# Three edits to a fused transformer kernel on one core: later transposed tokens in the inner pipeline, another job order in the first attention, a routing product over 128 rows

## The chip, the cores and the metric

The kernel runs on one core of one Trainium2 chip. A core has TensorE (PE, with its weight loads listed as PEld), VectorE (DVE), ScalarE (ACT), GpSimdE (POOL) and a queue for transfers (SP); each runs its own list of instructions in order and they wait for each other through semaphores. The metric is the device time in microseconds (us) of one execution, the median of three runs.

## The reference

Input `x` is 16 batches of 256 tokens by 128 features. All arithmetic is float32. Two outer layers are computed, each as `x = x + s * silu(g)` after a layernorm `xn` of `x`:

```
# layer 0
s = sliding_window_attention(xn)   # 16 heads of 8, window 64, each token sees its block of 64 and the one before, ALiBi-like bias
g = moe(xn)                        # 8 experts of 176, top 2 of a softmax router, plus a shared expert of 352: silu(x wg) * (x wu) @ wd
# layer 1
s = attention(xn)                  # 16 heads of 8, all 256 keys, a relative bias
g = inner(xn)                      # depth 2, each: shift tokens, local attention (8 heads of 64, window 64, rotary, l2-normed q and k),
                                   #   x = x + o @ wo;  h = layernorm(shift(x)) ; x = x + (a * gelu(b)) @ w2 + b2,  a, b = split(h @ w1)
```

## The kernel before

The program is a row of blocks, one after the other, each with an instruction list for every engine: `load_inputs`, `layernorm`, `router`, `head_attention("a0")`, `experts`, `layernorm`, `head_attention("a1")`, `inner_layers`, `finish`. At the end of a block the engines meet. The change touches three of them. In all three the order of every engine's work is written out by hand as a loop over steps, and `k` in "step s handles item s + k" is a lookahead.

**First attention (`a0`, windowed).** A batch of 256 tokens has two tiles of 128 tokens, and a tile has two units of 8 heads, so there are 4 steps a batch and 64 units in all. For each unit PE computes `score`, DVE adds the bias table (line 700) and takes row maxima (706), POOL subtracts them (508), ACT takes the exponent (667), PE transposes the probabilities (576), ACT copies them to SBUF (672), and PE sums values and denominators (602, 609). Scores run 4 units ahead, for two units in every even step. DVE normalises a tile (711, 713) in each odd step. Beside that stream stand small jobs that all go through one PSUM bank, bank 7: `x` (transpose the tokens of a batch, 532), `qk` (project queries and keys, 536), `v` (project values, 542) and one `y` for each tile (output projection, 547). Every job must have been copied out by ACT (643, 648, 649, 658, 662) before PE may begin the next one; this is `after(pe, aux_free, n)`. POOL expands the keys of a batch (`mask_keys`, 501) from ACT's copy before PE scores it. `x` and `qk` of a batch stand two batches ahead of its units. In an even step PE does `qk` or `v` ahead of `score`; `y` stands last in an odd step, so the next job, first in the following even step, comes right behind it.

**Experts.** 8 rounds of 512 tokens. The 1760 features are cut into 14 slices `s` (11 routed, 3 shared). For a slice PE does a gate product and an up product of three matmuls each (817, 818, 819: high and low parts in fp32r), then for the 11 routed slices one matmul (848) that spreads the routing weights `wT` (24 rows by 512 tokens, bf16) over the slice's features with the selection matrix `sel16` (24 rows by 1408). The down product of slice s-2, again three matmuls, follows. DVE multiplies (953, 957), ACT splits off the high part (919), POOL the low part (932) that the down product waits for. In slice 8 PE also transposes the next round's tokens (825), which ACT copies (890) ahead of its next high part; in slice 10 it transposes the next routing weights (831, 128 by 24 each), which ACT copies too (894). ACT makes `sel16` once, at the block's start (886).

**Inner layers.** 64 tile steps (2 layers of 32 tiles). In a step PE does `score` (1249), the query and key projection of the tile 5 ahead (1214 to 1216), `transpose_out` (1283), `transpose_prob` (1258), the value projection (1222 to 1224) after it has waited for DVE's `add_mask` of the same step, `tokens` (1202), `project_out` (1289), sometimes `mlp_out` (1312), `sums` (1273) and `transpose_qk` (1233), and at the end one chunk of the feed-forward's first product (1303). A feed-forward round R covers four tiles and is spread over the steps 4R+6 to 4R+13. In step 4R+7 DVE computes `deviations(R)` (1578 to 1585, the normalised tokens `mn`), PE transposes them at the very end of the same step (`mlp_tokens`, 1295, into bank 0), and DVE scales them into `mT` (`keep_mlp_tokens`, 1593), also in that step. In step 4R+8 the first chunk follows, last on PE. The query and key projection uses banks 0 and 1 too, and so waits for `m_sb`.

```
R, c = round_at(step, 8)          # PE, end of a step
if R is not None and c < NC:
    projections_taken(pe, step)
    if not is_tile(step + LEAD):
        banks_01_free(pe, step)
    mlp_chunk(R, c)
R, c = round_at(step, 7)
if R is not None and c == 0:
    ...
    mlp_tokens(R)
```

## Time and profile before

| | |
|---|---|
| median of 3 runs | 1960.74 us (1957.76 to 1961.09) |
| profiled execution | 1958.84 us, its span 1956.5 us |
| busy in the span | PE 1619.0 (83%), PEld 1187.8 (61%), DVE 1375.9 (70%), ACT 1183.4 (60%), POOL 1087.8 (56%) |
| DMA | 40.16 MB, mean 21 GB/s |

Read it by blocks, since their limits differ. Seen in the timeline, the first attention runs from 96 to 348 us, the experts from 348 to 678 us, the second attention from 701 to 1102 us and the inner layers from there to 1937 us. The span is one execution as the profiler saw it; the profiled execution's own time is some 2 us above it.

### The profile page before, as it was taken

How to read it: one execution, taken by the hardware profiler on the slowest of the kernel's cores; microseconds unless marked ns; L12 is line 12 of the kernel's file. 1: busy time of each engine (PE TensorE's matmuls, PEld its weight loads, DVE VectorE, ACT ScalarE, POOL GpSimd, SP SyncE). 2: the span in 40 equal slices, each digit the busy share in tenths (PEclk: the TensorE clock that was granted, in tenths of full speed). 3: DMA queues.
4: the chain of work that ended last, by engine and by line, in shares of the span. 5: the costliest groups of instructions: out<-in, count | busy, mean ns of one | idle time of the engine just before them, and what ended most of it. 6: DMA issues, size and time to landing. Idle time of an engine off the chain costs nothing. (4 is left out here: it accounts for less than half of the span.)

```text
span 1956.5 us, 47756 instructions
## 1 busy us (share of the span) xinstructions
PE 1619.0 (83%) x18705; PEld 1187.8 (61%) x18705; DVE 1375.9 (70%) x2187; ACT 1183.4 (60%) x1972; POOL 1087.8 (56%) x632
## 2 busy tenths in 40 slices
PE   0479999699999739999999668888888999888863
PEld 0346666466666527677777447666666777666742
DVE  4468887444554569999999588877777777777633
ACT  0147767444444327777777558777777777777742
POOL 0166665244444327777776677666666666666413
PEclk9999999899999959999999879999999998999986
DMA  3010000000000140000000001111111111111101
GB/s 104 2 48 3 3 3 3 14 13 7 6 7 6 29 133 2 2 2 2 3 2 2 10 15 32 23 23 23 23 24 24 23 23 23 23 26 24 23 21 43
DMA packets 52210, 40.16 MB, mean 21 GB/s; under 512 B 24408, under 2 KB 44028, under 8 KB 51876
## 3 DMA queue, kind: packets, MB, share of 16 engines
q1 hardware_dynamic: 52004, 37.28, 7.4%
q8 instruction: 145, 2.38, 0.5%
q14 instruction: 61, 0.50, 0.1%
HBM read 15.68 MB, written 2.13 MB: 9 GB/s over the span
## 5 line engine op out<-in xcount | busy, mean ns | idle before, releaser
L508 POOL TENSOR_TENSOR a_prob<-a_prob,a_top 128x1024 f32<-128x1024 f32 x192 | 359.7, 1894 | 133.1 <-DVE a_top L706 133.1
L700 DVE TENSOR_TENSOR a_prob<-ps,a_table 128x1024 f32<-128x1024 f32 x192 | 226.2, 1220 | 70.6 <-PE ps L562 47.8
L932 POOL TENSOR_TENSOR e_hh<-e_h,e_hh 128x512 fp32r<-128x512 f32 x112 | 144.2, 1290 | 195.4 <-ACT e_hh L919 193.7
L672 ACT ACTIVATE a_probT<-ps 128x1024 f32<-128x1024 f32 x192 | 196.5, 1023 | 90.0 <-PE ps L576 89.9
L706 DVE TENSOR_REDUCE a_top<-a_prob 128x4 f32<-128x1024 f32 (+1 forms) x192 | 225.2, 1215 | 8.7
L576 PEld LDWEIGHTS ps<-ident,a_prob 128*128 128x128 f32 x1536 | 168.0, 141 | 95.5 <-issue 60.1
L667 ACT ACTIVATE a_prob<-a_prob 128x1024 f32<-128x1024 f32 x192 | 202.7, 1056 | 33.0 <-POOL a_prob L508 33.0
L576 PE MATMUL ps<-ident,a_prob 128*128 128x128 f32 x1536 | 208.9, 279 | 7.8 <-ACT a_probT L672 2.9
L1170 POOL TENSOR_TENSOR i_qk<-i_qk,i_rn 128x1024 f32<-128x1024 f32 x64 | 123.3, 1927 | 117.7 <-DVE i_rn L1498 117.7
L1157 POOL TENSOR_TENSOR i_qk<-i_raw,i_rot 128x1024 f32<-128x1024 f32 x64 | 152.0, 2375 | 47.8 <-issue 42.6
L953 DVE TENSOR_TENSOR e_h<-ps,e_sg 128x512 f32<-128x512 f32 x112 | 77.4, 691 | 143.7 <-PE ps L819 118.3
L902 ACT ACTIVATE e_sg<-ps 128x512 f32<-128x512 f32 x112 | 66.9, 597 | 160.0 <-PE ps L819 160.0
L1412 ACT ACTIVATE i_prob<-i_prob,i_top 128x128 f32<-128x128 f32 x512 | 156.3, 394 | 9.8 <-DVE i_top L1507 8.0
L1160 POOL TENSOR_TENSOR i_qk<-i_qk,i_rt 128x1024 f32<-128x1024 f32 x64 | 151.3, 2365 | 19.4 <-DVE i_rt L1515 12.4
L602 PE MATMUL ps<-a_probT,a_V 128*32 128x64 f32 (+1 forms) x4096 | 159.5, 250 | 1.7 <-DVE a_oT L713 1.5
L1377 ACT ACTIVATE i_raw<-ps 128x1024 f32<-128x1024 f32 x64 | 65.6, 1025 | 154.5 <-PE ps L1216 154.4
L609 PE MATMUL ps<-a_probT,a_ones 128*32 128x128 f32 x3072 | 154.3, 273 | 0.0
L602 PEld LDWEIGHTS ps<-a_probT,a_V 128*32 128x32 f32 x4096 | 90.6, 109 | 33.7 <-issue 31.0
L501 POOL TENSOR_TENSOR a_kM<-a_kT,a_own 128x1024 f32<-128x1024 f32 x32 | 60.6, 1894 | 69.9 <-ACT a_kT L651 52.7
L817 PE MATMUL ps<-e_xT,e_wgu_hi 128*128 128x512 f32 x224 | 91.3, 408 | 4.7 <-DVE e_wd_lo L977 4.7
L1515 DVE TENSOR_TENSOR i_rt<-ps,i_rot 128x512 f32<-128x512 f32 x128 | 82.1, 683 | 15.1 <-ACT i_raw L1377 14.9
L1303 PE MATMUL ps<-i_mT,i_w 128*128 128x512 f32 (+1 forms) x192 | 90.6, 594 | 2.2 <-DVE i_A L1600 2.2
(213 smaller groups left out, 3830.9 us busy)
## 6 DMA issues: line engine op xcount, KB each, us to landing
i_V<-i_V SPq DMA_DIRECT2D x96, 130.0 KB, 2.3
a_table<-skew_scratch SPq DMA_DIRECT2D x2, 2048.0 KB, 12.9
X<-in_L_attn_x SPq DMA_DIRECT2D x4, 512.0 KB, 6.3
a_table<-in_c_l_table SPq DMA_DIRECT2D x1, 2048.0 KB, 8.1
e_xs<-Y SPq DMA_DIRECT2D x8, 256.0 KB, 2.3
i_ms<-Y SPq DMA_DIRECT2D x16, 128.0 KB
out_dram<-X SPq DMA_DIRECT2D x4, 512.0 KB, 3.3
i_ms<-Y SPq DMA_DIRECT2D x16, 127.0 KB
```

What stands on the lines that cost most here:

```text
L508: nc.gpsimd.tensor_tensor(s, s, top[:, slot].unsqueeze(2).broadcast_to([P, HG, KW]), ALU.subtract).then_inc(shifted, 1)
L576: last = nc.tensor.transpose(ps[:, 4 + b // 4, (b % 4) * P:(b % 4 + 1) * P], flat[:, b * P:(b + 1) * P], ident[:, :])
L602: nc.tensor.matmul(ps[32 * g:32 * g + 32, 6, cols], vals[:, 32 * x:32 * x + 32], src[:, at + cols.start:at + cols.stop], start=(first and ...
L609: last = nc.tensor.matmul(ps[32 * g:32 * g + 32, 6, P:2 * P], ones[:].rearrange("p x d -> p (x d)")[:, 32 * x:32 * x + 32], src[:, at:at + ...
L667: nc.scalar.activation(s, s, ACT.Exp).then_inc(exped, 1)
L672: nc.scalar.activation(probT[:, n % 4].rearrange("p (b n) -> p b n", b=2), ps[:, 4:6, :], ACT.Copy).then_inc(pT_sb, 1)
L700: nc.vector.tensor_tensor(prob[:, slot].rearrange("p (b x) k -> p b x k", b=2), ps[:, 2 * (n % 2):2 * (n % 2) + 2, :].rearrange("p b (x k) ...
L706: nc.vector.tensor_reduce(top[:, slot], prob[:, slot], AX.X, ALU.max).then_inc(max_done, 1)
L932: nc.gpsimd.tensor_tensor(hh[0:n, b % HBUF, 1, :], h[0:n, b % HBUF, :], hh[0:n, b % HBUF, 0, :].bitcast(F32), ALU.subtract).then_inc(h_lo, 1)
L1157: nc.gpsimd.tensor_tensor(s, raw[:, T % 2], cosines, ALU.mult).then_inc(cos_done, 1)
L1160: nc.gpsimd.tensor_tensor(s, s, rt[:], ALU.add).then_inc(rotated, 1)
L1412: last = nc.scalar.activation(s, s, ACT.Exp, bias=top[:, T % 2, h:h + 1])
```

## The change

**First attention.** The shared function is split in two, `window_attention` for `a0` and `bias_attention` for `a1`; the latter issues what it did. In `window_attention` the jobs `x` and `y` become one job `xy` in each batch's slot for `x`: it transposes the tokens of batch i and does the output projection of both tiles of batch i-4, in different halves of bank 7. ACT copies both, the second as one piece of 256 columns. `oT` has four buffers in place of two. In a step, PE now does `score` ahead of the job, and ACT the exponent ahead of the job's copies.

**Experts.** `ws`, `wT` and `sel16` are 128 rows (or columns) wide in place of 24, the rest of them zero; POOL clears `ws` and `sel16` at the block's start, and the first transfers and ACT's copy wait for that. The routing product is over 128 rows, of which 104 are zero. `ws` is filled by the same transfers, now into strided rows.

**Inner layers.** `mlp_tokens` moves from the end of step 4R+7 to step 4R+8, between `mlp_out` and `sums`; `keep_mlp_tokens` moves on DVE to step 4R+8, between `add_mlp` and `quotient`. The wait of the next projection for `m_sb` goes.

```diff
+def window_attention(nc, name, t, ps, ident, Y, S):
...
-        oT = sb("oT", [P, 2, P])
+        oT = sb('oT', [P, 4, P])
...
-        AT = {"x": -7, "qk": -6, "v": 0} if windowed else {"x": -7, "qk": -6, "v": -3}
-        JOBS = sorted([(i * U + AT[kind], 0, kind, i, 0) for i in range(NBATCH) for kind in AT]
-                      + [((T + 1) * NU + 3, 1, "y", T // TPB, T % TPB) for T in range(TILES)])
+        AT = {'xy': -7, 'qk': -6, 'v': 0}
+        DELAY = 4
+        LAST = (NBATCH + DELAY - 1) * U + AT['xy'] + 1
+        JOBS = sorted([(i * U + AT[kind], kind, i) for i in range(NBATCH) for kind in AT] + [(i * U + AT['xy'], 'xy', i) for i in range(NBATCH, NBATCH + DELAY)])
...
+                if kind == 'xy':
+                    if i < NBATCH:
+                        for k in range(TPB):
+                            last = nc.tensor.transpose(ps[:, 7, k * P:(k + 1) * P], Y[:, i * TPB + k, :], ident[:, :])
+                    if i >= DELAY:
+                        for k in range(TPB):
+                            T = (i - DELAY) * TPB + k
+                            pe.wait_ge(o_sb, T + 1)
+                            last = nc.tensor.matmul(ps[:, 7, (2 + k) * P:(3 + k) * P], oT[:, T % 4, :], wT[:, 3, :], start=True, stop=True)
...
+            for step in range(FIRST, LAST):
+                if step % 2 == 0 and 0 <= step + AHEAD < UNITS:
+                    score(step + AHEAD)
+                for n, kind, i in jobs_at(step):
+                    job(n, kind, i)
+                if 0 <= step < UNITS:
+                    transposes(step)
+                if 0 <= step - 2 < UNITS:
+                    sums((step - 2) // 2, step % 2)
...
-        sel16 = sb("sel16", [3 * NE, ROUTED], BF16)
+        sel16 = sb("sel16", [P, ROUTED], BF16)
-        ws = sb("ws", [P, 4, 3 * NE])
+        ws = sb("ws", [P, 4, P])
-        wT = sb("wT", [3 * NE, 2, N], BF16)
+        wT = sb("wT", [P, 2, N], BF16)
...
-                sp.dma_start(ws[:], wparts[:, bass.ds(i * 4, 4), :]).then_inc(staged, 16)
-
+                sp.dma_start(ws[:, :, 0:3 * NE], wparts[:, bass.ds(i * 4, 4), :]).then_inc(staged, 16)
+
+            sp.wait_ge(cleared, 2)
...
+            nc.gpsimd.memset(ws[:], 0.0).then_inc(cleared, 1)
+            nc.gpsimd.memset(sel16[:], 0.0).then_inc(cleared, 1)
...
-            R, c = round_at(step - 1, 7)
-            if R is not None and c == 0:
-                eng.wait_ge(m_sb, R + 1)
...
+                R, c = round_at(step, 8)
+                if R is not None and c == 0:
+                    projections_taken(pe, step)
+                    if not is_tile(step + LEAD):
+                        banks_01_free(pe, step)
+                    mlp_tokens(R)
                 if is_tile(step - 1):
                     sums(step - 1)
...
-                R, c = round_at(step, 7)
-                if R is not None and c == 0:
-                    projections_taken(pe, step)
-                    if not is_tile(step + LEAD):
-                        banks_01_free(pe, step)
-                    mlp_tokens(R)
...
+                R, c = round_at(step, 8)
+                if R is not None and c == 0:
+                    keep_mlp_tokens(R)
                 if is_tile(step - 1):
                     quotient(step - 1)
```

PE in the first attention before, at the middle of the batches: `a_wT,a_oT` is a `y`, `a_xT,a_wT` a `qk`, `a_kM,a_qT` a score, `ident,a_prob` the transposed probabilities, the last two names the sums.

```order
L609 MATMUL ps<-a_probT,a_ones 32x128 x4
L547 MATMUL ps<-a_wT,a_oT 128x128
L536 MATMUL ps<-a_xT,a_wT 128x256 x2
L562 MATMUL ps<-a_kM,a_qT 64x512 x8
L576 MATMUL ps<-ident,a_prob 128x128 x8
L602 MATMUL ps<-a_probT,a_V 32x64 x8
```

The `xy` job on PE in the changed kernel (`ident,Y` and `a_wT,a_oT` with two products), with the step's transposes and the first of its sums behind it.

```order
L505 MATMUL ps<-ident,Y 128x128 x2
L510 MATMUL ps<-a_wT,a_oT 128x128 x2
L539 MATMUL ps<-ident,a_prob 128x128 x8
L559 MATMUL ps<-a_probT,a_V 32x64 x8
L563 MATMUL ps<-a_probT,a_ones 32x128 x4
```

The `qk` job in the next step of the changed kernel, between the last sum of the step ahead and the first of its own.

```order
L563 MATMUL ps<-a_probT,a_ones 32x128 x4
L531 MATMUL ps<-a_kM,a_qT 64x512 x8
L513 MATMUL ps<-a_xT,a_wT 128x256 x2
L539 MATMUL ps<-ident,a_prob 128x128 x8
L559 MATMUL ps<-a_probT,a_V 32x64 x8
```

The output projection no longer stands right before another job: transposes, sums and a score lie between `xy` and `qk`.

PE in the inner layers before, from the end of step 4R+7 (`ident,i_G` is `mlp_tokens`) into step 4R+8; `i_qkT` is the score, `i_mT,i_w` the feed-forward's chunk.

```order
L1289 MATMUL ps<-i_wo,i_oT 128x128 x4
L1273 MATMUL ps<-i_V,i_probT 64x65 x16
L1233 MATMUL ps<-ident,i_qk 128x128 x8
L1295 MATMUL ps<-ident,i_G 128x128 x4
L1249 MATMUL ps<-i_qkT 64x128 x16
L1214 MATMUL ps<-i_w_hi,i_h_hi 128x512
```

The end of step 4R+8 on PE in the changed kernel.

```order
L1494 MATMUL ps<-i_wo,i_oT 128x128 x4
L1517 MATMUL ps<-i_w,i_A 128x128 x6
L1500 MATMUL ps<-ident,i_G 128x128 x4
L1478 MATMUL ps<-i_V,i_probT 64x65 x16
L1438 MATMUL ps<-ident,i_qk 128x128 x8
L1508 MATMUL ps<-i_mT,i_w 128x512 x2
```

`mlp_tokens` has moved past the score, both projections, `transpose_out`, `transpose_prob`, `project_out` and `mlp_out` of the next step, and stands two groups ahead of the chunk that needs it.

DVE in the same steps, in the changed kernel, from the last of `deviations` (`i_G`) over `add_mask` (`i_prob`) to the scaled tokens (`i_mT`), which stood right behind `i_G` before.

```order
L1790 TENSOR_SCALAR i_G<-i_ms,i_mv,i_rstd 128x128 x4
L1699 SCALAR_TENSOR_TENSOR i_rtmp<-i_ss,i_rn 128x32
L1701 TENSOR_TENSOR i_rtmp<-i_rtmp,i_rn 128x32
L1703 SCALAR_TENSOR_TENSOR i_rn<-i_rtmp,i_rn 128x32
L1728 TENSOR_REDUCE i_ss<-i_sq 128x16
L1709 TENSOR_TENSOR i_prob<-ps,i_mask 128x1024
L1712 TENSOR_REDUCE i_top<-i_prob 128x8
L1720 TENSOR_TENSOR i_rt<-ps,i_rot 128x512 x2
L1749 CAST i_h_hi<-ps 64x128
```

Behind these stand three more writes of the token parts, the two additions to `Y`, and then `i_mT`, ahead of the reciprocal of `quotient`.

## Rows read from the trace of the kernel before

**Rows 1.** Busy time by stretch: start:end, length, then busy us (instructions) of each engine, PEclk, DMA share, GB/s.

```profile
96.00:348.00 252.00, 225.53 (x4388) 157.14 (x4388) 187.76 (x192) 164.17 (x274) 155.55 (x88) 0.99 0.04 12
...
363.00:676.00 313.00, 296.91 (x1181) 196.08 (x1181) 151.77 (x221) 138.11 (x246) 144.22 (x112) 0.99 0.02 6
...
1140.00:1900.00 760.00, 659.95 (x7067) 523.15 (x7067) 572.35 (x1163) 560.76 (x1082) 464.59 (x244) 0.95 0.11 24
```

**Rows 2.** Timeline of PE and ACT, first attention: start, us, engine, line [idle before].

```profile
202.46 1.16 PE L542 MATMUL ps<-a_wT,a_xT 128*128 128x128 f32 x8 [0.37 <-ACT S L662]
...
216.12 0.49 PE L547 MATMUL ps<-a_wT,a_oT 128*128 128x128 f32 x2
216.64 0.28 ACT L662 ACTIVATE S<-ps 128x128 f32<-128x128 f32 x1 [0.41 <-PE ps L547]
...
216.97 1.16 PE L542 MATMUL ps<-a_wT,a_xT 128*128 128x128 f32 x8 [0.37 <-ACT S L662]
...
218.06 1.11 PE L562 MATMUL ps<-a_kM,a_qT 32*64 32x512 f32 x16
```

**Rows 3.** Timeline of DVE in the same two steps.

```profile
214.49 2.35 DVE L706 TENSOR_REDUCE a_top<-a_prob 128x8 f32<-128x1024 f32 x2
...
216.75 0.95 DVE L711 RECIPROCAL a_rden<-ps 128x128 f32<-128x128 f32 x1
...
217.77 0.29 DVE L713 TENSOR_TENSOR a_oT<-ps,a_rden 128x128 f32<-128x128 f32 x1
...
219.28 2.36 DVE L700 TENSOR_TENSOR a_prob<-ps,a_table 128x1024 f32<-128x1024 f32 x2 [1.22 <-PE ps L562]
```

**Rows 4.** Timeline of PE around a routing product of the experts.

```profile
382.66 0.39 PE L819 MATMUL ps<-e_xT,e_wgu_lo 128*128 128x512 f32 x1
...
382.98 0.39 PE L848 MATMUL ps<-e_wT,e_sel 24*128 24x512 bf16 x1
...
383.29 0.50 PE L817 MATMUL ps<-e_hh,e_wd_hi 128*128 128x512 f32 x1
...
383.63 0.39 PE L818 MATMUL ps<-e_hh,e_wd_hi 128*128 128x512 f32 x1
```

**Rows 5.** Timeline of PE and PEld, inner layers, fp32r to float32 of equal shape.

```profile
1428.39 0.39 PE L1224 MATMUL ps<-i_w_hi,i_h_lo 128*128 128x512 f32 x1
1428.39 0.14 PEld L1202 LDWEIGHTS ps<-ident,Y 128*128 128x128 f32 x1
...
1428.62 0.27 PE L1202 MATMUL ps<-ident,Y 128*128 128x128 f32 x1
```

**Rows 6.** Timeline of PE, experts: the down product of slice 9.

```profile
389.11 0.50 PE L817 MATMUL ps<-e_hh,e_wd_hi 128*128 128x512 f32 x1 [0.16 <-POOL e_hh L932]
```

**Rows 7.** Groups by line, 1140 to 1900 us: count, busy, mean ns, idle before.

```profile
L1295 PE MATMUL ps<-ident,i_G 128*128 128x128 f32 x60 | 13.1, 357 | 53.4 <-DVE i_G L1585 53.4
```

**Rows 8.** Timeline of PE and DVE, inner layers, into and through step 4R+8.

```profile
1411.13 0.68 PE L1295 MATMUL ps<-ident,i_G 128*128 128x128 f32 x4 [4.21 <-DVE i_G L1585]
1411.74 1.99 PE L1249 MATMUL ps<-i_qkT 64*64 64x128 f32 x32
1411.85 0.81 DVE L1593 TENSOR_SCALAR i_mT<-ps,i_vecs 128x512 f32<-128x512 f32 x1 [0.86 <-PE ps L1295]
...
1414.52 1.21 DVE L1504 TENSOR_TENSOR i_prob<-ps,i_mask 128x1024 f32<-128x1024 f32 x1
...
1416.98 0.48 PE L1222 MATMUL ps<-i_w_hi,i_h_hi 128*128 128x512 f32 x1
...
1420.46 0.28 DVE L1544 CAST i_h_hi<-ps 64x128 fp32r<-64x128 f32 x1 [2.17 <-PE ps L1312]
...
1421.96 0.41 DVE L1606 TENSOR_TENSOR Y<-ps,Y 128x256 f32<-128x256 f32 x1
...
1422.21 1.88 PE L1303 MATMUL ps<-i_mT,i_w 128*128 128x512 f32 x4
```

**Rows 9.** Timeline of PE after a shorter wait, inner layers.

```profile
1153.12 0.50 PE L1222 MATMUL ps<-i_w_hi,i_h_hi 128*128 128x512 f32 x1 [2.53 <-DVE i_prob L1504]
```

More of the change, by code:

```diff
@@ L380, in _ @@
                     dve.drain()
[L383 to L385 removed]
+def window_attention(nc, name, t, ps, ident, Y, S):
+    KW = 2 * WIN
     HG = 1024 // KW
@@ L439, in jobs_at @@
-        def jobs_at(step, place):
-            return [(n, kind, i, tile) for n, (s, p, kind, i, tile) in enumerate(JOBS) if (s, p) == (step, place)]
-        def job_of(kind, i, tile=0):
-            return [j[2:] for j in JOBS].index((kind, i, tile)) + 1
+        sb = lambda n, s: c.enter_context(nc.sbuf_tensor(name + '_' + n, s, F32))
+        sem = lambda n: c.enter_context(nc.semaphore(name + '_' + n))
+        wnat = sb('wnat', [P, 4, P])
+        wT = sb('wT', [P, 4, P])
+        own = sb('own', [P, QG])
@@ new lines, in _, with add_bias, row_max, normalise @@
+        @block.vector
+        def _(dve):
+            dve.wait_ge(b_loaded, NBL)
+            dve.wait_ge(zeroed, NZERO)
+            def add_bias(n, slot):
+                i, tile, pair, half = unit(n)
+                dve.wait_ge(scores, n // 2 + 1)
+                after(dve, p_T, n - NBUF + 1)
+                heads = table[:, tile].rearrange('p (g x) k -> p g x k', x=QG)
+                nc.vector.tensor_tensor(prob[:, slot].rearrange('p (b x) k -> p b x k', b=2), ps[:, 2 * (n % 2):2 * (n % 2) + 2, :].rearrange('p b (x k) -> p b x k', k=KW), heads[:, 2 * half:2 * half + 2, XX * pair:XX * (pair + 1), :], ALU.add).then_inc(biased, 1)
+            def row_max(n, slot):
+                nc.vector.tensor_reduce(top[:, slot], prob[:, slot], AX.X, ALU.max).then_inc(max_done, 1)
+            def normalise(T):
+                dve.wait_ge(pv, (T + 1) * NU)
+                after(dve, aux_ps, job_of('xy', T // TPB - 2 + DELAY) if T >= 4 else 0)
+                nc.vector.reciprocal(rden[:, :], ps[:, 6, P:2 * P])
+                dve.drain()
+                nc.vector.tensor_tensor(oT[:, T % 4, :], ps[:, 6, 0:P], rden[:, :], ALU.mult).then_inc(o_sb, 1)
+                dve.drain()
+            def job(n, kind, i):
+                dve.wait_ge(aux_ps, n + 1)
+                split = lambda a: a.rearrange('p (g x d) -> p g x d', g=4, x=QG)
+                for k in range(TPB):
+                    last = nc.vector.tensor_tensor(V[:, i % 2, 0, k, :, :, 0:D], split(ps[:, 7, k * P:(k + 1) * P]), split(bvo[:, 0, :]), ALU.add)
+                last.then_inc(aux_free, 1)
+            for step in range(FIRST, LAST):
+                T, r = divmod(step - 1, NU)
+                n = step + AHEAD
+                if r == 0 and 1 <= T <= TILES:
+                    normalise(T - 1)
+                if step % 2 == 0 and 0 <= n < UNITS:
+                    add_bias(n, n % NBUF)
+                    add_bias(n + 1, (n + 1) % NBUF)
+                dve.drain()
+                if step % 2 == 0 and 0 <= n < UNITS:
+                    row_max(n, n % NBUF)
+                    row_max(n + 1, (n + 1) % NBUF)
@@ L540, in job @@
                             at = PAD + P * k - WIN * v
[L541 to L543 removed]
+                            rows = xR[:, par, at:at + P]
+                            last = nc.tensor.matmul(ps[:, 7, (v * TPB + k) * P:(v * TPB + k + 1) * P], rows, wT[:, 2, :], start=True, stop=True)
                 else:
@@ L682, in _ @@
                     keep_probT(step)
-                if windowed:
-                    for n, kind, i, tile in jobs_at(step, 1):
-                        job(n, kind, i, tile)
         @block.vector
@@ L730, in _ @@
                     normalise(T - 1)
-                if not windowed:
-                    for a, kind, i, tile in jobs_at(step, 1):
-                        job(a, kind, i, tile)
+                for a, kind, i, tile in jobs_at(step, 1):
+                    job(a, kind, i, tile)
                 n = step + AHEAD
@@ L737, in _ @@
                     add_bias(n + 1, (n + 1) % NBUF)
-                if not windowed:
-                    for a, kind, i, tile in jobs_at(step, 0):
-                        if kind == "v":
-                            job(a, kind, i, tile)
+                for a, kind, i, tile in jobs_at(step, 0):
+                    if kind == 'v':
+                        job(a, kind, i, tile)
                 dve.drain()
```

442 lines of the change are left out of this document (289 added, 153 removed).

## The prediction

> **What bounds the kernel now.** I began with the page: PE is busy 83% of the span, no other engine above 70%. The chain that ended last says little here, since its rows cover 1% of the span. So I asked for busy time by stretch [rows 1] and then read the timeline inside each block that the change touches. In the first attention PE is busy 225.53 of 252.00 us and in the experts 296.91 of 313.00, both at a granted clock of 0.99. DVE, the next one, has 187.76 and 151.77. These blocks go at PE's pace, and what is to be looked for is time that PE loses between its instructions. In the inner layers PE has 659.95 of 760.00 us at a clock of 0.95; there it waits for others at certain places, and one has to find who sets the end of a round of four steps.
>
> **First attention: the end of a wait.** `y` starts at 216.12, ACT copies it at 216.64 for 0.28 us, and PE's next job `v` starts at 216.97 [rows 2]. From start to start that is 0.85 us. The four products of `v` take 216.97 to 218.06, 0.27 us each, and `y` is one product of that kind. So 0.58 us are a wait for one copy, in every odd step, ahead of `v` or `qk`. In the changed order a whole step's transposes and sums lie behind `xy`, and a score too, so the copy is hidden. `y`'s two products stay. Of the 32 `y` jobs 27 have a job right behind them (tiles 0 to 25 and 27); the batch period, 202.46 to 216.97, is 14.51 us and should become 14.51 - 2 x 0.58 = 13.35.
>
> Does another engine stop that? DVE needs for two steps 2.36 + 2.35 + 0.95 + 0.29 us and about 0.1 of gaps, 6.05 us in all, and now waits 1.22 us for scores [rows 3]. The batch of 13.35 us holds two such pairs, 12.1, so DVE fits with 1.2 us left. The pair with `qk` is the shorter one on PE (it has no `xy`), about 6.4 us: still over 6.05. POOL has 155.55 us of 252 [rows 1] and fits. What gets later is the key expansion: `qk` now stands behind a score (some 1.1 us, [rows 2]), and the scores that need the keys stand first in their step and no longer behind the 1.09 us of `v`. That eats about 2.2 us of a lead of a whole pair of steps less POOL's expansion, so I cost it at nothing in the steady part, but at the start, where PE has no lead, at 1.4 us. The last `xy` adds a product and a longer copy, 0.4 us. Sum: 27 x 0.58 - 1.8 = 13.9; **-14 us**. Bounds: the waits come back in part as waits of DVE's kind, -6; nothing is lost at the start and the gaps between array shapes shrink as well, -18.
>
> **Experts: the routing product.** A stream of 512-column matmuls runs at 0.23 us from start to start, as 1428.39 to 1428.62 shows [rows 5]. Around the routing product it is 382.66, 382.98, 383.29, 383.63 [rows 4]: 0.97 us for three, where 0.69 would do. 0.28 us are lost each time. Nothing is waited for; the load for the routing product starts only when the stream ahead is through, and so does the next one's. Which property of it does that, the 24 rows or bf16? Rows 5 show a change of type at equal shape, fp32r to float32: the load of 1202 starts at 1428.39, together with the matmul ahead of it, and costs nothing. Rows 4 differ from that in shape and in bf16. I take the shape, with bf16 as the open part: no row has a bf16 product over 128 rows. There are 8 x 11 = 88 such products: 88 x 0.28 = 24.6 us.
>
> The Trainium skill has a rule on each side. TensorEngine Tiling (Array Packing), Tiling Modes, says that a change of tiling mode, not just of tile, drains the engine, and 24 rows fall in a mode of 32; by it the whole 24.6 us go, and rows 4 agree. TensorE: Matmul & The Clock Gate, section LDWEIGHTS, says that a load with 32 rows takes as long as one with 128 and that only columns count; read alone, it makes the edit worth 0. That is a rival below.
>
> Some of it is given back where PE then meets POOL's low part. The down product of slice 9 waits 0.16 us already [rows 6]: ACT copies the next tokens ahead of its high part, and this copy depends on PE's transposes in slice 8. They stand right behind a routing product, so they come only 0.32 + 0.31 - 2 x 0.23 = 0.17 us earlier, while the down product would come 2 x 0.28 = 0.56 earlier. I take 0.4 us a round there, 0.2 for the like of it with the routing weights in slice 10 and 11 (the transposes of 128 columns in place of 24 included), over 7 rounds 4 us. The two clears at the start, the strided transfer and ACT's wait for the clears cost nothing: from the block's start at 348 to the first product at 363 [rows 1] the engines split the expert weights, and the tokens are wanted only behind that. Should that cover be gone, they cost some 2 us, once. Sum: **-21 us**, bounds 0 and -25.
>
> **Inner layers: the moved transposes.** PE stood 53.4 us before line 1295 in 15 rounds, waiting for DVE [rows 7]. It is tempting to book them all. Rows 8 show one round. `mlp_tokens` starts at 1411.13 after a wait of 4.21. DVE then scales at 1411.85 for 0.81, and only at 1412.66 goes on with the norms and square sums of the next step; `add_mask` is over at 1415.73, and the value projection, which needs it, starts at 1416.98. With the edit DVE goes on at 1411.1, so `add_mask` is over at 1415.73 - 1.55 = 1414.2. PE has the score, the projection and both transposes behind it long before (they were free from 1407 on; 4 us of work at full clock) and waits for `add_mask` in place of the tokens. So the value projection starts at 1414.3 in place of 1416.98, 2.65 us earlier. DVE's part of it (1544 at 1420.46, 1606 at 1421.96 to 1422.37) follows at the same distance: over at 1419.7. Now comes what was put off: the scaled tokens take 0.81 us more here, to 1420.6, and the chunk at 1422.21 needs them. PE itself is ready at 1422.21 - 2.65 + 0.5 (the transposes put in) = 1420.1. The chunk starts at 1420.7: 1.5 us gained a round, and DVE's `quotient` behind it gains as much. 15 rounds: **-22 us**. Bounds: -40 if the scaled tokens are no limit (2.65 x 15); 0 if the chunk's wait and the later `quotient` eat it.
>
> **The sum** is -14 - 21 - 22 = -57 us against the profiled execution's 1958.84, that is 1901.8. The median of the runs shown, 1960.74, lies 1.9 above it: 1903.7, say **1904 us**.
>
> **Rivals.**
> 1. *The routing product gains nothing*, because bf16 or the length of a load is what costs, not the rows. For it: no row shows bf16 at 128 rows. Against it: rows 5. 1904 + 21 = 1925 us.
> 2. *The inner wait only moves.* PE's 4.21 us turn into the wait for `add_mask` plus the one for the scaled tokens, and the round keeps its length. For it: the chunk is within 0.6 us of a DVE-set time in my own account. 1904 + 22 = 1926 us.
> 3. *Slower, through the clock.* The wait of 4.21 us is followed by a score of 1.99 us [rows 8], at the lower level, 1.2 GHz; a wait of 2.53 us is followed by a matmul of 0.50 us, still at 2.4 GHz [rows 9]. In the changed step PE waits some 2.6 us for `add_mask`, right ahead of the longest stretch of products on the path. If that wait drops the clock, value projection to chunk, 1422.21 - 1416.98 + 0.5 = 5.7 us at full clock, doubles: 5.7 - 1.5 = 4.2 us lost a round, +63. With the other blocks' -35 that is 1961 + 28 = 1989 us. It turns the kernel slower from a loss of 35 / 15 = 2.3 us a round on.
> 4. *The inner round gains the full 2.65*, or more as the clock stays up: 1904 - 18 = 1886 us.
>
> **How the numbers follow.** The forecast, all three parts within a few us (1890 to 1915), 0.55; rival 1 0.14; rival 2 0.14; rivals 1 and 2 together (1947) 0.02; rival 3 0.05; rival 4 0.10. About 0.2% (4 us) is what a measurement of this kernel can tell from no change. The range goes from 1885 to 1927 and leaves out the double failure, rival 3 and some of the ends: below 0.2. Faster by over 0.2%: all but rival 3 and a bit of the double failure, 0.94; same 0.01; slower 0.05. The forecast's own range is 1890 to 1915.
>
> **What the changed profile would show.** First attention: `v` and `qk` without an idle ahead of them, and a batch of 13.3 to 13.5 us; if 14 or more, look at DVE ahead of its bias addition and at PE ahead of the score, for the keys. Experts: 0.23 us on both sides of the routing product, and a wait of about 0.5 us for POOL in slice 9; if 0.32 stays, rival 1 holds. Inner layers: no wait before the token transposes, one of 2 to 3 us before the value projection of step 4R+8, and about 0.5 before the chunk; a round of 46.5 us. If the value projection there has matmuls well above the 0.48 us of rows 8, the clock has dropped, and rival 3 is at work. The prediction is wrong if a block's gain is missing, which each of these rows tells by itself.

## The result, and the profile after

The changed kernel takes 1907.31 us (median of 4 runs, 1906.76 to 1909.29), the one before 1960.91 (4 runs beside it): ratio 0.9732, 95% interval 0.9715 to 0.9748. The profiled execution took 1909.29 us with a span of 1907.2.

The blocks follow from where each one's first instruction stands in the two traces: the first attention is 17.7 us shorter, the experts 19.8, the layer norm and second attention 0.5 longer, the inner layers 12.1 shorter. Sum 49.1 of the spans' 49.3. The forecast had 14, 21 and 22.

Busy time by stretch of the kernel after, the answer to [rows 1] (start:end, length, busy us and instructions of PE, PEld, DVE, ACT, POOL, clock, DMA share, GB/s):

```profile
96.00:330.00 234.00, 215.68 (x4388) 156.78 (x4388) 189.11 (x192) 161.97 (x258) 155.02 (x88) 1.00 0.04 13
345.00:639.00 294.00, 276.87 (x1168) 198.37 (x1183) 151.73 (x222) 140.04 (x246) 144.03 (x112) 0.99 0.02 7
1103.00:1863.00 760.00, 659.29 (x7084) 521.72 (x7085) 576.55 (x1179) 567.02 (x1087) 467.56 (x246) 0.96 0.11 24
```

In the inner layers PE is as busy in 760 us as before. A shorter round should have put more work into them.

**First attention**, timeline of PE in the kernel after, against [rows 2]:

```profile
203.69 0.40 PE L563 MATMUL ps<-a_probT,a_ones 128*32 128x128 f32 x8
204.02 1.11 PE L531 MATMUL ps<-a_kM,a_qT 32*64 32x512 f32 x16
205.07 1.13 PE L513 MATMUL ps<-a_xT,a_wT 128*128 128x256 f32 x4
206.03 1.04 PE L539 MATMUL ps<-ident,a_prob 128*128 128x128 f32 x8
...
211.28 1.16 PE L518 MATMUL ps<-a_wT,a_xT 128*128 128x128 f32 x8
...
214.26 0.44 PE L505 MATMUL ps<-ident,Y 128*128 128x128 f32 x2
214.53 0.61 PE L510 MATMUL ps<-a_wT,a_oT 128*128 128x128 f32 x4
```

No wait stands ahead of `qk` (L513), `v` (L518) or the joint job (L505 and L510). The score stands right behind the sums, and the job right ahead of the transposes. From score to score a batch takes 6.21 + 6.74 = 12.95 us. It was 14.51, and the forecast said 13.35.

**Experts**, timeline of PE around a routing product (L1052) in the kernel after, with that product's load (PEld), against [rows 4]:

```profile
351.70 0.40 PE L1023 MATMUL ps<-e_xT,e_wgu_lo 128*128 128x512 f32 x1
351.93 0.10 PEld L1052 LDWEIGHTS ps<-e_wT,e_sel 128*128 128x128 bf16 x1 [0.28 <-issue]
351.94 0.39 PE L1052 MATMUL ps<-e_wT,e_sel 128*128 128x512 bf16 x1
351.98 0.58 PE L1021 MATMUL ps<-e_hh,e_wd_hi 128*128 128x512 f32 x1
352.39 0.40 PE L1022 MATMUL ps<-e_hh,e_wd_hi 128*128 128x512 f32 x1
```

From L1023 to L1022 it is 0.69 us, where the same three gaps took 0.97 before. How they split (0.24, 0.04, 0.41) is odd, but the sum is that of an unbroken stream, as forecast. The load of the routing product still starts only with its own product (351.93 beside 351.94) and not with the one ahead of it, so a load that is not issued ahead is not enough to cost time. The wait for POOL in slice 9, forecast at about 0.5 us, is 0.25 (0.16 before). The give-back that it was to explain came all the same: an undisturbed round of 14 slices went from 38.84 to 36.40 us, 2.44 where eleven routing products save 11 x 0.27 = 3.0. Where the difference goes was not traced.

**Inner layers**, timeline of PE through a step 4R+8 of the kernel after, against [rows 8]; the first two lines are from the same place one round earlier:

```profile
1232.54 1.06 PE L1494 MATMUL ps<-i_wo,i_oT 128*128 128x128 f32 x8
1233.43 1.50 PE L1517 MATMUL ps<-i_w,i_A 128*128 128x128 f32 x12
...
1277.87 0.50 PE L1427 MATMUL ps<-i_w_hi,i_h_hi 128*128 128x512 f32 x1 [2.38 <-DVE i_prob L1709]
...
1278.94 1.92 PE L1494 MATMUL ps<-i_wo,i_oT 128*128 128x128 f32 x8
1280.65 2.16 PE L1517 MATMUL ps<-i_w,i_A 128*128 128x128 f32 x12
...
1285.77 1.95 PE L1508 MATMUL ps<-i_mT,i_w 128*128 128x512 f32 x4 [0.42 <-DVE i_mT L1798]
```

The two waits are those forecast: 2.38 us for the mask's addition (2.6 forecast) and 0.42 for the scaled tokens (0.5). But the output projection and `mlp_out` take 1.92 and 2.16 us. One round earlier they took 1.06 and 1.50. Windows over the 3 us behind the value projection's start in the two rounds, the granted clock third from the end:

```profile
1231.60:1234.60 3.00, 2.97 (x23) 2.79 (x24) 2.42 (x3) 1.68 (x6) 2.38 (x2) 1.00 0.00 0
1277.87:1280.90 3.03, 3.03 (x14) 2.80 (x15) 2.42 (x3) 1.74 (x6) 2.38 (x2) 0.62 0.00 0
```

At a granted clock of 1.00, which is 2.4 GHz, the trace has 23 PE instructions; at 0.62, so mostly at 1.2 GHz, it has 14. A round of the first kind takes 46.2 us, one of the second 47.8, and before it was 47.95. Of the twelve rounds behind the first one, 10 were of the long kind. So the shift that the forecast described is there, and the clock, rival 3 of the forecast, eats nearly all of it in most rounds. The stretch from the first score to the last got 7.7 us shorter; the other 4.4 lie behind the last score (67.3 against 62.9 us), where the same code took 66.6 us in another kernel below. In the main that part is the clock as well, and not a gain of the edit. Behind the last score PE waits 3.2 us for ACT in each kernel, and the output projection behind that wait runs at either level. Timeline of PE, the kernel after and then the kernel with idle products that is shown below:

```profile
1829.87 1.13 PE L1494 MATMUL ps<-i_wo,i_oT 128*128 128x128 f32 x8 [3.22 <-ACT i_oT L1628]
...
1814.58 2.04 PE L1494 MATMUL ps<-i_wo,i_oT 128*128 128x128 f32 x8 [3.21 <-ACT i_oT L1632]
```

The granted clock in the 3 us from there is 1.00 in the first and 0.50 in the second. In the kernel before it is 0.63 in the like place.

### The profile page after: what moved, and what is told of

It reads as the page before. It is cut to its first block and busy times, and to the rows that moved or that the text cites. A ratio compares the mean times of both kernels' runs of the same rounds, so it can differ in the third digit from the quotient of the medians.

```text
span 1907.2 us, 47691 instructions
## 1 busy us (share of the span) xinstructions
PE 1585.1 (83%) x18689; PEld 1184.5 (62%) x18705; DVE 1377.3 (72%) x2187; ACT 1185.4 (62%) x1956; POOL 1088.5 (57%) x634
## 3 DMA queue, kind: packets, MB, share of 16 engines
q8 instruction: 145, 2.38, 0.5%
## 5 line engine op out<-in xcount | busy, mean ns | idle before, releaser
L888 ACT ACTIVATE a_probT<-ps 128x1024 f32<-128x1024 f32 x128 | 131.0, 1024 | 71.6 <-PE ps L817 71.6
L913 DVE TENSOR_REDUCE a_top<-a_prob 128x4 f32<-128x1024 f32 x128 | 150.1, 1215 | 5.8
L883 ACT ACTIVATE a_prob<-a_prob 128x1024 f32<-128x1024 f32 x128 | 134.8, 1053 | 29.1 <-POOL a_prob L761 29.1
L817 PEld LDWEIGHTS ps<-ident,a_prob 128*128 128x128 f32 x1024 | 111.8, 141 | 62.0 <-issue 35.8
L817 PE MATMUL ps<-ident,a_prob 128*128 128x128 f32 x1024 | 139.1, 279 | 4.5 <-ACT a_probT L888 1.2
L837 PE MATMUL ps<-a_probT,a_V 128*32 128x128 f32 x2048 | 105.9, 279 | 0.5 <-DVE a_oT L920 0.4
L841 PE MATMUL ps<-a_probT,a_ones 128*32 128x128 f32 x2048 | 102.9, 273 | 0.0
```

The source lines that it names most:

```text
L817: last = nc.tensor.transpose(ps[:, 4 + b // 4, b % 4 * P:(b % 4 + 1) * P], flat[:, b * P:(b + 1) * P], ident[:, :])
L883: nc.scalar.activation(s, s, ACT.Exp).then_inc(exped, 1)
L888: nc.scalar.activation(probT[:, n % 4].rearrange('p (b n) -> p b n', b=2), ps[:, 4:6, :], ACT.Copy).then_inc(pT_sb, 1)
L913: nc.vector.tensor_reduce(top[:, slot], prob[:, slot], AX.X, ALU.max).then_inc(max_done, 1)
```

## Experiments

Times are medians. The kernel before took 1959.3 to 1961.1 us beside them. Four questions are asked: do the parts stand alone, what costs at the routing product, what is the first attention's order worth, and what holds the inner round.

### Each part alone

The kernel before, with only the code of one part taken over.

> The kernel before with the first attention's new code alone; experts and inner layers as before. Theory (the three parts are independent, and the traces before and after show the first attention 17.7 us shorter): 1960.9 - 17.7 = 1943 us, with 12.95 us a batch in place of 14.51. Rival (part of what the block shows is a shift that later blocks give back, or take): more than 3 us away from 1943.

> The kernel before with the routing product over 128 rows alone. Theory (0.28 us lost at each of 88 products, a little of it given back at slices 9 to 11; the traces show the experts 19.8 us shorter): 1960.9 - 19.8 = 1941 us. Rival (the saving of the experts needs the first attention's new order ahead of it, or the product gains nothing by itself): 1955 to 1961 us.

> The kernel before with the token transposes and their scaling moved by one step alone. Theory (independent parts, the traces show the inner layers 12.1 us shorter, as the wait for the mask's addition drops the clock in most rounds): 1960.9 - 12 = 1949 us, with the output projection at some 1.9 us in most rounds in place of 1.06. Rival (the clock drops only by chance of this execution): 1960.9 - 22 to - 25, 1936 to 1939 us, with the output projection at 1.06 in most rounds.

Measured: first attention alone 1943.3 us (1938.7 to 1946.6; ratio 0.9889 to 0.9935), routing product alone 1937.7 (0.9868 to 0.9901), inner move alone 1941.5, with a wide spread (1937.2 to 1948.9; 0.9879 to 0.9939). In the profiles the first attention's batch is as in the full change, the experts are 22.2 us shorter, and the inner layers 15.9 us, with 5 long rounds of 12 in place of 10. Each part gives its gain in its own block; the sum of the three, 17 + 22 + 19 = 58 us, is 5 more than they give together. In the profiles the inner layers alone give 3.8 us more than in the full change (15.9 against 12.1), as the count of long rounds is not the same in each kernel; the experts alone give 2.4 more (22.2 against 19.8) and the first attention 1.2 (18.9 against 17.7). For the inner part neither expectation held: it is a mixture of both.

### The routing product: rows or type

```diff
-        sel16 = sb("sel16", [P, ROUTED], BF16)
-        wT = sb("wT", [P, 2, N], BF16)
+        sel16 = sb("sel16", [3 * NE, ROUTED], F32R)
+        wT = sb("wT", [3 * NE, 2, N], F32R)
...
```

> The changed kernel with the routing product over 24 rows again, but in fp32r like its neighbours. Theory (the shape costs, not the type): the 0.28 us at each of 88 products are back, 1907 + 20 = 1927 us, and PE shows 0.31 to 0.34 us on both sides of the routing product. Rival (bf16 next to fp32r costs): 1907 us or a little less, 0.23 us on both sides.

```diff
-   nc.tensor.matmul(ps[:, 4 + s % 2, :], sel16[:, a:a + n], wT[:, parity, :], ...)
+   nc.tensor.matmul(ps[:, 4 + s % 2, :], sel16[0:64, a:a + n], wT[0:64, parity, :], ...)
```

> The changed kernel with the routing product over 64 of the 128 rows, in bf16. Theory (any change of the row shape between neighbours costs): 1927 us. Rival (only a product in 32 rows or fewer costs): 1907 us. Second rival (the cost goes with how far the rows differ): between them.

Measured: 24 rows in fp32r 1938.0 us, 64 rows in bf16 1921.6. Timeline of PE, 24 rows in fp32r:

```profile
392.13 0.39 PE L1023 MATMUL ps<-e_xT,e_wgu_lo 128*128 128x512 f32 x1
392.45 0.49 PE L1052 MATMUL ps<-e_wT,e_sel 24*128 24x512 f32 x1
392.87 0.50 PE L1021 MATMUL ps<-e_xT,e_wgu_hi 128*128 128x512 f32 x1
393.20 0.39 PE L1022 MATMUL ps<-e_xT,e_wgu_hi 128*128 128x512 f32 x1
```

Timeline of PE and its loads, 64 rows in bf16:

```profile
387.66 0.40 PE L1022 MATMUL ps<-e_xT,e_wgu_hi 128*128 128x512 f32 x1
387.67 0.19 PEld L1023 LDWEIGHTS ps<-e_xT,e_wgu_lo 128*128 128x128 f32 x1
387.90 0.40 PE L1023 MATMUL ps<-e_xT,e_wgu_lo 128*128 128x512 f32 x1
...
388.23 0.09 PEld L1052 LDWEIGHTS ps<-e_wT,e_sel 64*128 64x128 bf16 x1 [0.37 <-DVE e_h L1165]
388.23 0.39 PE L1052 MATMUL ps<-e_wT,e_sel 64*128 64x512 bf16 x1
...
388.54 0.19 PEld L1021 LDWEIGHTS ps<-e_xT,e_wgu_hi 128*128 128x128 f32 x1 [0.23 <-issue]
388.55 0.50 PE L1021 MATMUL ps<-e_xT,e_wgu_hi 128*128 128x512 f32 x1
```

Between equal shapes the next load starts with the running product (387.67 beside 387.66). At a change of shape it starts only 0.3 us later, and so does the load behind. Three gaps take 0.97 us with 24 rows, 0.98 with 64 and 0.69 with 128: both changes of the row shape cost the same 0.28, and at 128 rows bf16 between fp32r products costs nothing. fp32r makes it worse, 0.32 + 0.42 + 0.33 = 1.07 us. Its load takes 0.18 us where bf16's takes 0.09, and at a change of shape that load lies open. 88 x 0.38 = 33 us; the inner layers start at 1095.6 us here and at 1064.8 in the changed kernel, 31 us later. In the kernel with 64 rows the experts are 22 us longer than with 128, but the whole only 14, because its inner layers had 5 long rounds. By the time alone one would have taken this for "between", the second rival; the block tells the theory apart.

TensorEngine Tiling (Array Packing), Tiling Modes, in the Trainium skill, says that changing the tiling mode drains the engine, and lists 64 and 32 rows as modes of their own. The traces agree: 24 rows and 64 rows each cost 0.28 us next to 128, and 128 next to 128 nothing.

### The first attention's order

The joint job stays, and score and exponential stand behind the jobs again.

```diff
-                if step % 2 == 0 and 0 <= step + AHEAD < UNITS:
-                    score(step + AHEAD)
                 for n, kind, i in jobs_at(step):
                     job(n, kind, i)
+                if step % 2 == 0 and 0 <= step + AHEAD < UNITS:
+                    score(step + AHEAD)
...
```

> The changed kernel with the first attention's joint job for tokens and output kept, but the jobs of a step ahead of the score on PE and ahead of the exponential on ACT again, as before. Theory (the gain comes from the output products no longer standing ahead of v and qk, not from the order of score and job): 1907 us within 3, a batch of 12.9 to 13.1 us. Rival (the score first is what hides the copy of the token transposes, which qk wants one step later, and keeps the keys on time): up to the whole 17.7 us lost, 1925 us; a batch of up to 14.5.

Measured: 1900.3 us (1899.7 to 1903.0), 7 less than the changed kernel. But the first attention itself takes as long (236.0 against 236.1 us, first transfer to first transfer); the 7 us are the inner layers, 6 long rounds in place of 10. The equal time hides two terms. In the steady part a batch takes 6.38 + 6.86 = 13.24 us against 12.95, a little over the 12.9 to 13.1 expected, and far from the rival's 14.5. The score first saves 0.29. The traces show where: from a job to the transposes it is 0.96 or 0.99 us, where from a job to a score it was 1.06 or 1.09, and from the transposes to the sums 0.97 in place of 1.02. That it is because score and sums are both narrow shapes, and job and transposes both full ones, fits but was not separated. At the start the score first costs as much. Groups that waited, timeline of PE, first the changed kernel:

```profile
107.90 2.01 PE L531 MATMUL ps<-a_kM,a_qT 32*64 32x512 f32 x16 [2.54 <-POOL a_kM L470]
112.43 2.01 PE L531 MATMUL ps<-a_kM,a_qT 32*64 32x512 f32 x16 [1.90 <-DVE a_prob L631]
118.93 2.01 PE L531 MATMUL ps<-a_kM,a_qT 32*64 32x512 f32 x16 [2.49 <-POOL a_kM L470]
...
126.79 0.69 PE L531 MATMUL ps<-a_kM,a_qT 32*64 32x512 f32 x8
```

then the one with the jobs first:

```profile
108.02 2.01 PE L531 MATMUL ps<-a_kM,a_qT 32*64 32x512 f32 x16 [2.54 <-POOL a_kM L470]
113.13 2.01 PE L531 MATMUL ps<-a_kM,a_qT 32*64 32x512 f32 x16
117.73 1.12 PE L531 MATMUL ps<-a_kM,a_qT 32*64 32x512 f32 x16 [0.94 <-DVE a_prob L631]
123.43 1.11 PE L531 MATMUL ps<-a_kM,a_qT 32*64 32x512 f32 x16
```

The fourth score stands at 126.79 in the one and 123.43 in the other. Part of that is this execution: the third spacing, 118.93 to 126.79 = 7.86 us, is 6.83 in the second profile of the same kernel, whose first attention is 1.4 us shorter.

### The inner round: is it the clock

```diff
+                    if R is not None and c == 0:
+                        for _ in range(8):
+                            nc.tensor.transpose(ps[:, 7, 3 * P:4 * P], ident[:, :], ident[:, :])
                     after(pe, masked, step + 1)
                     project_v(step + 1)
```

> The changed kernel with 8 transposes of the identity into an unused corner of PSUM, nobody reads them, put ahead of the value projection in each step 4R+8, where PE waits 2.38 us for the mask's addition. They take 8 x 0.11 to 0.27 us in that wait. Theory (the wait drops the clock to 1.2 GHz, and output projection and mlp_out then take 1.92 + 2.16 us in place of 1.06 + 1.50, so the chunk starts 7.9 in place of 6.3 us behind the value projection): with PE busy the clock stays, 1.6 us gained in each of 12 to 13 rounds, 1907 - 20 = 1887 us. Rival (these products are slow for another reason, such as PSUM or the loads, and the clock's row only goes with it): 1907 us, or some us more where the fillers end behind the mask's addition. Second rival (the next round's wait takes the gain back): steps 4R+8 get shorter by 1.6 and 4R+9 to 4R+11 longer, 1907 us.

Measured: 1897.6 us (1896.9 to 1898.1). Timeline of PE:

```profile
1275.81 1.04 PE L1538 MATMUL ps<-ident 128*128 128x128 f32 x8
1278.36 0.50 PE L1427 MATMUL ps<-i_w_hi,i_h_hi 128*128 128x512 f32 x1 [1.51 <-DVE i_prob L1713]
...
1279.26 1.05 PE L1494 MATMUL ps<-i_wo,i_oT 128*128 128x128 f32 x8
1280.15 1.50 PE L1517 MATMUL ps<-i_w,i_A 128*128 128x128 f32 x12
...
1284.62 1.96 PE L1508 MATMUL ps<-i_mT,i_w 128*128 128x512 f32 x4 [0.42 <-DVE i_mT L1802]
```

Products that nobody reads, 0.9 us of them in a wait, make the kernel 10 us faster. All twelve rounds take 46.1 to 46.6 us (from score to score); the chunk starts 6.26 us behind the value projection, and 7.90 in the changed kernel's round above. The window behind the value projection, clock third from the end, has 23 PE instructions again:

```profile
1278.36:1281.36 3.00, 3.00 (x23) 2.83 (x24) 2.42 (x3) 1.71 (x6) 2.38 (x2) 1.00 0.00 0
```

From first to last score it is 698.2 us against 713.5, so 15.3 us, which is 10 rounds of 1.6. Against the kernel before (721.2 us) it is 23 us, so with the clock held the moved transposes give what was forecast for them, 22. The clock is shown as the cause, and a wait of 1.51 us with PE busy ahead of it was followed by no drop in this run. The total gained less than the 20 expected, since there were 10 long rounds and not 12 to 13, and since the part behind the last score took 4 us more (67.0).

Is the number of long rounds chance?

> The changed kernel once more, unchanged. In its first runs 11 of 13 inner rounds took 47.8 us and 2 took 46.2 to 46.6; the same inner layers behind other blocks had 5 to 7 of the long ones. Theory (how many rounds lose the clock hangs on how the rounds lie, which the blocks ahead set, and little on chance): 1907 us within 1.5, 10 or more long rounds. Rival (chance from one execution to the next): anything from 1897 to 1909 us.

Measured: 1906.3 us; three of four runs within 0.7 us, one at 1901.0. The profile has 9 long rounds, other ones than the first time. It is neither fixed nor free: the kernel stays near its value, but single executions fall out.

The six profiles with this inner code unaltered (the kernel after twice, the inner move alone, 24 rows in fp32r, 64 rows, jobs first) have 72 such rounds between them, and they say more. In 16 of them the wait ahead of the value projection is only 1.72 to 1.78 us, and none of these is a long round. In the other 56 it is 2.08 to 2.40 us; 41 of these are long and 15 are not. So a wait of this length makes the drop likely, not certain.

### What DVE is late for

The mask's addition is DVE's, so the question is why DVE comes 2.4 us after PE. Timeline of DVE and POOL in the changed kernel:

```profile
1270.68 2.36 POOL L1365 TENSOR_TENSOR i_qk<-i_qk,i_rt 128x1024 f32<-128x1024 f32 x1 [0.16 <-issue]
1271.02 2.04 DVE L1783 SCALAR_TENSOR_TENSOR i_mtmp<-i_var,i_rstd 128x4 f32<-128x4 f32 x1
```

An instruction on 4 elements takes 2.04 us, and ends where POOL's ends (1273.06 and 1273.04). In the kernel before it is the same (2.02, median of 16). Both read two tensors from SBUF. The edit puts the variance and the intermediate values into an unused corner of PSUM (and has PE wait for the variance ahead of the sums that use that bank):

```diff
+        scratch = ps[:, 7, 3 * P:3 * P + 8]
...
+                nc.vector.tensor_scalar(scratch[:, 0:4], mv[:, :, 1], 1e-5, None, ALU.add)
...
-                nc.vector.scalar_tensor_tensor(mtmp[:], var[:], -0.5, rstd[:], ALU.mult, ALU.mult)
+                nc.vector.scalar_tensor_tensor(tmp, v, -0.5, rstd[:], ALU.mult, ALU.mult)
...
-                nc.vector.scalar_tensor_tensor(rstd[:], mtmp[:], 1.5, rstd[:], ALU.add, ALU.mult)
+                nc.vector.scalar_tensor_tensor(rstd[:], tmp, 1.5, rstd[:], ALU.add, ALU.mult)
...
```

> The changed kernel with the refinement of the inner layers' reciprocal deviation working on values in PSUM, so that none of its three small instructions on DVE reads two tensors from SBUF; a fourth small instruction writes the variance there. The trace of the changed kernel has the first of the three at 2.04 us for 128x4 elements in every round where it starts while POOL runs a rotary addition, and it ends when that ends (1271.02 + 2.04 = 1273.06; 1270.68 + 2.36 = 1273.04). Theory (DVE waits there for POOL's instruction, since both read two tensors from SBUF): 0.2 us in place of 2.04, the mask's addition 1.8 us earlier, PE's wait of 2.38 us down to about 0.6, the clock stays up, 1.8 + 1.6 = 3.4 us a round, 15 rounds, 1907 - 50 = 1857 us. Rival (the time is the wait for ACT's seed or a start-up of this instruction, and POOL's end is a coincidence): still 2.04 us, 1907 us. Second rival (the instruction is short, but the next one, the norms' refinement, waits for the same end): 0 to 0.5 us a round, 1900 to 1907 us.

Measured: 1883.8 us (1882.8 to 1884.1; ratio 0.9592 to 0.9629), 23.5 less than the changed kernel. Timeline of DVE and PE:

```profile
1270.48 0.16 DVE L1789 SCALAR_TENSOR_TENSOR ps<-ps,i_rstd 128x4 f32<-128x4 f32 x1
...
1275.52 0.50 PE L1428 MATMUL ps<-i_w_hi,i_h_hi 128*128 128x512 f32 x1 [0.98 <-DVE i_prob L1713]
```

The instruction takes 0.16 us, PE's wait is 0.98 in place of 2.38, and every round takes 45.3 to 45.8 us. The theory holds for place and cause. The size was half of what was expected, as something like the second rival had a part, though not at the instruction that it named: in 8 of the 16 rounds the next DVE instructions, the scalings of the staged tokens (one tensor read from SBUF, one written), now take 2.2 us for four in place of 1.12. That is seen again in the next kernel. Most of the gain came through the clock: a round that had held it goes from 46.2 to 45.4 us, 0.8 less, and a long one from 47.8, 2.4 less.

The rounds of the unaltered inner code bear the cause out. In those with a wait of 1.7 us in place of 2.4, the first of the three small instructions takes only 0.9 to 1.3 us in place of 2.04: it starts 1.1 to 1.5 us behind POOL's addition and not 0.3, and ends with it, within 0.03 us, all the same.

The Trainium skill, SBUF — State Buffer, section Who interferes with whom, says that a DVE instruction with two SBUF inputs contends with a GpSimd instruction that reads SBUF, that one in a two-port mode (which `tensor_scalar`, the scaling here, can enter) contends with GpSimd, and that whoever issues first keeps the shared ports for its whole instruction. The 2.04 us above agree for the first kind, and the scalings (1.45 us in place of 0.34, shown further down) fit the second; no run shows in which mode they were.

The next edit takes the square sums from ahead of the mask's addition in even steps:

```diff
-                if is_tile(step + LEAD - 1):
+                if step % 2 and is_tile(step + LEAD - 1):
                     square_sums(step + LEAD - 1)
                 if is_tile(step):
                     add_mask(step)
+                if step % 2 == 0 and is_tile(step + LEAD - 1):
+                    square_sums(step + LEAD - 1)
```

> The kernel with the refinement in PSUM (1883.8 us), and in even steps of the inner layers the square sums on DVE behind the mask's addition and the row maxima. In its trace PE still waits 0.98 us for the mask's addition in step 4R+8, the square sums of 1.22 us stand right ahead of that, and DVE then idles 1.04 us for mlp_out's product. Theory (the round is set by DVE to the mask's addition, then PE to mlp_out, then DVE to the scaled tokens): the 0.98 us of PE and as much of the 1.04 us of DVE go, a round of 45.42 - 1.0 = 44.4 us, 15 rounds, 1884 - 15 = 1869 us. Rival (the square sums are then late for ACT's square buffer or POOL's clip, or DVE's later instructions for the chunk): 1880 us or more.

Measured: 1869.7 us, as the theory had it; the rounds take 43.9 to 44.4 us. And with the first attention in both orders (jobs ahead of the score up to step 3):

> The kernel before this one, and in the first attention the jobs ahead of score and exponential up to step 3, the score first from step 4 on. Theory (score first saves 0.29 us a batch in the steady part, 12.95 against 13.24 us, and costs 4.3 us once at the start, where the first steps take 6.50 and 7.86 in place of 4.60 and 5.70 us): both advantages, the first attention 4 us shorter, 232 us from its first transfer to the experts' in place of 236, and with the round of 44.4 us in all 1865 us. Rival (the start's loss only moves to the step where the order changes): 1869 us, the first attention at 236.

Measured: 1865.0 us (1859.3 to 1867.5; ratio 0.9483 to 0.9523), the first attention at 231.7 us in place of 235.9. This beats both kernels. Timeline of DVE and POOL in the kernel of 1869.7 us:

```profile
1267.78 2.37 POOL L1366 TENSOR_TENSOR i_qk<-i_qk,i_rt 128x1024 f32<-128x1024 f32 x1 [0.16 <-issue]
...
1268.78 1.45 DVE L1796 TENSOR_SCALAR i_G<-i_ms,i_mv,i_rstd 128x128 f32<-128x128 f32 x1
```

The last kernel cuts POOL's addition in two, in one step of four:

```diff
-                nc.gpsimd.tensor_tensor(s, s, rt[:], ALU.add).then_inc(rotated, 1)
+                if (T - LEAD - 7) % 4:
+                    nc.gpsimd.tensor_tensor(s, s, rt[:], ALU.add).then_inc(rotated, 1)
+                else:
+                    nc.gpsimd.tensor_tensor(s[:, 0], s[:, 0], rt[:, 0], ALU.add)
+                    nc.gpsimd.tensor_tensor(s[:, 1], s[:, 1], rt[:, 1], ALU.add).then_inc(rotated, 1)
```

> The fastest kernel so far (refinement in PSUM, mask's addition first, first attention in both orders, 1865.0 us), with POOL's rotary addition of 2.36 us in step 4R+7 of the inner layers cut into two instructions of half the size. In its trace the first of the four scalings of the staged tokens on DVE, one tensor read from SBUF and written there, takes 1.4 us in place of 0.34 in many rounds and ends with POOL's addition (1268.78 + 1.45 = 1270.23; 1267.78 + 2.37 = 1270.15): the wait taken from the refinement has moved here, 514 ns mean over 64 in place of 341, 11 us in all. Theory (DVE's instruction waits for the whole of POOL's instruction and gets its turn between two): the wait falls to what is left of the first half, 0.2 us or less in place of 1.1, some 0.7 us a round in 15 rounds, 1865 - 10 = 1855 us. Rival (the turn is only had when POOL's queue is empty, or POOL's later instructions lose what DVE gains): 1865 us or a little more.

Measured: 1866.7 us (1862.5 to 1867.4), so nothing. Timeline of POOL and DVE:

```profile
1264.45 1.27 POOL L1376 TENSOR_TENSOR i_qk<-i_qk,i_rt 128x512 f32<-128x512 f32 x1 [0.16 <-issue]
1265.46 0.35 DVE L1807 TENSOR_SCALAR i_G<-i_ms,i_mv,i_rstd 128x128 f32<-128x128 f32 x1
...
1265.46 1.59 DVE L1807 TENSOR_SCALAR i_G<-i_ms,i_mv,i_rstd 128x128 f32<-128x128 f32 x2
...
1265.68 1.28 POOL L1377 TENSOR_TENSOR i_qk<-i_qk,i_rt 128x512 f32<-128x512 f32 x1
```

(The first scaling alone, then the first two together, of two windows.) The first goes through at the end of one half, as the theory wants; the second is over at 1265.46 + 1.59 = 1267.05, just behind the other half (1265.68 + 1.28 = 1266.96). In the 8 rounds where it shows, the four scalings take 2.1 us together, and took 2.2 with the addition in one piece. My reading is that DVE gets one turn at each end of a POOL instruction; no run varied the number of pieces further.

## Why the prediction was right, and where its sizes were not

- **The total**, 1904 for 1907.3, is better than its terms, and in that it was lucky: the first attention gave 3.7 us more, the experts 1.2 less, the inner layers 10 less than forecast. Of what the inner layers gave, 4.4 us lie behind the last score and are the clock of that execution. The blocks sum to 49 us and the medians differ by 54, since the profiled execution of the kernel after is the slowest of its four and that of the kernel before lies 2 us under its median.
- **First attention, -14 forecast, -17.7 measured.** The mechanism is right: no wait ahead of `v` and `qk`. The term that was mis-sized is the batch. The joint job alone is worth 14.51 - 13.24 = 1.27 us (1.16 forecast), and the score ahead of the job another 0.29, which the forecast had only in a bound ("the gaps between array shapes shrink as well"). The loss at the start was put at 1.4 us; it is 3 to 4, as the run with the jobs first and the kernel with both orders show (its first attention is 4.2 us shorter than that of the kernel it builds on, 3.0 shorter than that of the changed kernel's second profile).
- **Experts, -21 forecast, -19.8 measured**, and -21.0 in the profile with jobs first, which has the same experts but no round of them at the lower clock; the kernel before and the kernel after each have one, some 1.5 us longer than the others. The choice of shape over type is shown by 64 rows, by fp32r and by the 128 rows in bf16 themselves. Rival 1 had it worth 0. Loads of 24, 64 and 128 rows in bf16 do all take 0.09 to 0.10 us, and TensorE: Matmul & The Clock Gate, section LDWEIGHTS, in the Trainium skill says the same of 32 and 128; but what costs is not the load's length. With fewer rows the routing product and the one behind it each start 0.31 to 0.33 us behind the product ahead of them. The clears at the start cost nothing: the first product stands 14.5 us behind the block's start, before and after.
- **Inner layers, -22 forecast, -12.1 measured.** The term that was mis-sized is "1.5 us gained a round", where the stretch from value projection to chunk was taken at full clock. Where the clock holds, a round gains 47.95 - 46.2 = 1.7 us; where it drops, 0.1. The forecast had this as rival 3 with a chance of 0.05 and a loss of 4.2 us a round, from a stretch that runs at 1.2 GHz throughout. In fact the lower clock lasts 3.4 us there, over the output projection and most of `mlp_out`, and costs 1.6 us. So the rival's mechanism was at work in 10 of 12 rounds, at less than half its price. So the chance of 0.05 was far too low for the mechanism, and the kernel did not get slower only because the stretch at 1.2 GHz was short. Rival 2, that the wait only moves, is refuted by the rounds at full clock, and by the run with idle products, whose rounds all hold it and gain 23 us together.
- **Rival 4** (the full 2.65 us) did not come: the scaled tokens hold the chunk for 0.42 us.

## What to carry to other kernels

When a wait of some 2.4 us is moved to stand ahead of PE's longest chain of products, count the drop to 1.2 GHz behind it as a term (1.6 us a round in 41 of 56 rounds here), not as a remote rival; idle products in the wait or a shorter wait are both remedies. Then ask why the releasing engine is late: a tiny DVE instruction with an odd duration was the cause here, and removing that was worth as much as the whole inner part was meant to give, two thirds of it through the clock. Compare blocks, not totals: the same inner code took 814 to 822 us in different kernels, and in the first attention an equal time hid two opposite terms of 4 us.

## What the hardware showed that was not expected

- A DVE instruction on 4 elements takes 2.04 us when it starts under a POOL instruction of 2.36 us that reads SBUF, and 0.16 with one operand in PSUM. A scaling of 128 elements goes from 0.34 to 1.45 us in the same way.
- The load of 128 columns takes 0.09 us in bf16 and 0.18 in fp32r. At a change of row shape the longer load shows, 0.38 us lost a product in fp32r against 0.28 in bf16, so that a narrower type matters just there.
- Which rounds lose the clock differs between executions of one kernel, and how many between kernels with the same inner code: 10, 9, 6, 6, 5 and 5 of 12. Rounds with a wait of 1.7 us never lost it. What sets the number among the longer waits stays open; no run here varied it by itself.
